# A Mamba-like block with a mixture of experts: the router's mean in halves, eight tokens normalised by ScalarE, and batch 0's LN turned by quarters

## The chip, the cores and the metric

The kernel runs on one core of a Trainium2 chip. The time is the device time of one execution in microseconds (us), the median of several runs. The engines are TensorE (PE, with its weight loads PEld), VectorE (DVE), ScalarE (ACT), GpSimd (POOL), and SyncE (SP), which issues the DMAs. Each engine runs its own instructions in their order; semaphores (`wait_ge`, `then_inc`) tie them together.

## The reference

Two batches (B = 2) of S = 2048 tokens, DM = 256, inner width DI = 512, H = 32 heads, all float32. Cut to what matters:

```python
xn   = rmsnorm(layernorm(x)) * rms_w
z, K, V = split(xn @ in_proj_W.T + in_proj_b)          # V: 512 wide, K: 512 x 2
u    = silu(causal_conv4(V) + conv_b)
coefficients = f(u @ dyn_W, seldt_W, selB, selC, beta, rg, ug)   # 11 x 32 columns per token
S_t  = rotate(S_{t-1}) + beta * (v - k . rotate(S_{t-1})) * k     # a scan over the tokens
y    = groupnorm(sum(Q * S_t)) * silu(z) + D * u
x1   = x + layernorm(layernorm(x) + y @ out_W.T)
# the experts, two of eight for each batch
x2   = layernorm(x1)
top2 = top_k(mean_over_tokens(x2) @ Wr, 2);  w = softmax(top2)
out  = x1 + layernorm(sum_e w_e * (gelu(x2 @ W1_e + b1_e) @ W2_e + b2_e))
```

## The kernel before

**Layout.** Token 16c + j of a batch lies in partition c, column j: a batch is L = 16 tiles j of 128 tokens, four of which make a quarter n (NCH = 4). V and u lie transposed in `uT`, four groups g of 128 channels; a "tile of V" is one (n, g), 512 columns, NV = 16 of them, made in the order VORD, which begins with quarters 3 and 0 of group 0, because the causal taps of quarter 0 need the last columns of quarter 3.

**Batch 0's start.** DVE makes the first statistics (`x_stats`) and in `normed_x` (L1219) centres and scales each token tile into `x_c`; PE turns it (two 128x128 transposes, L486); ACT evicts the first half of the channels (L826) and DVE the second (L1236). PE's `values` (L489) waits until all is turned. ACT's `values_and_u` (L839) evicts each tile of V twice (tap 3 of the convolution into `uT`, V itself into `vbuf`); DVE adds taps 2, 1 and 0 (`convolution`, L1263); ACT takes SiLU (`silu_u`); PE multiplies each token tile by 352 columns (`head_projections`, L528), and DVE evicts these head tiles (`head_tile`, L1313), 0 to 7 inside the convolution's loops and 8 to 15 as `tile(0)` to `tile(7)` inside `heads_half`.

**Work for batch 1 done ahead, in batch 0.** DVE takes statistics of batch 1's x (`x_ahead`), ACT the two roots (`root_ahead`), normalises the tiles (ACT's `x_ahead`), PE turns them and makes V (`values_ahead`, L502), ACT evicts (`turned_ahead` L883, `v_ahead` L890); both go to memory and come back when batch 1 starts. Where these steps stand in ACT's order is written out by hand in ACT's `heads` (L926), between the steps of the head arithmetic that DVE waits for. `fixed_steps` (L921) is softplus of a constant row; `key_bias` (L829) writes the bias of a key into its psum banks.

**Heads and scan.** DVE's `heads_half` (L1332) runs twice and hands square roots, logarithms and the like to ACT through `hd_vec` and `hd_act`. `pass_1` (L1515) goes through 16 keys backwards with 2 x 2 updates; PE makes the keys (`key`, L553) and turned tokens (`token_u`, L542). `chunk_scan` joins the 128 chunks; `turn_ends` (L592) and `turn_starts` (L614) turn its input and output on PE; `pass_2` (L1709) goes forward with the queries.

**Output and router.** `gates_and_norms` (ACT L1020, DVE L1789) gates y by quarters, adds the projection, takes the LN, adds x, and takes the next LN's statistics; ACT takes the roots (`block_root`), DVE normalises (`normed`, L1846). `mean_x2` (L703) sums x2 over the tokens on PE as a product of 1/std with x1. `router` (L720) turns x2 on PE in between; ACT evicts the turned tiles (L1065); DVE's `choose` (L1887) picks the experts and `expert_weights` (L1901) makes their softmax and copies it to all partitions (`wbc`).

**Experts.** Batch b's 64 expert units (NF; one is `up`, L746, four passes of 512 columns, with a Gelu of ACT, L1089, and `down`, L760, eight passes of 256) are spread: batch 0's run in the gaps of batch 1's attention, at places named by the constants UF = 4, UM = 7, US = 9, UH = 12 and the list UNITS; after `turn_ends` the units from UNITS[16] to 63 follow, and then the queries. Batch 1's 64 units end the kernel. SP loads the weights of two units at a time into a ring of four, in the order of the same constants. PE's order at the end of batch 1's scan:

```python
                keys(b)
                turn_ends(b)
                if b > 0:
                    experts(b - 1, UNITS[L], NF)
                    pe.wait_ge(f_used, b * NCH)
                queries(b)
```

## Time and profile before

| | us |
|---|---|
| median of 3 runs | 1499.26 (1498.65 to 1499.3) |
| the profiled execution | 1499.28 |
| its span, first to last instruction | 1497.2 |
| PE busy | 1263.3 (84%) |
| DVE busy | 1170.8 (78%) |
| ACT busy | 528.0 (35%) |
| POOL busy | 174.0 (12%) |
| mean granted TensorE clock | 0.943 of full |

Stages by the timeline: batch 0's projections and heads to about 156 us, its scan and queries to 543, its output and router to 614; batch 1's the same to 735, 1185 and 1256; batch 1's experts to 1487, and the last normalisation. A row of the timeline gives the start, the busy time of a group of like instructions, engine, line and operation, output and input, and in brackets the engine's idle time before it and what ended that. The profile ascribes a wait to the semaphore that came last.

### The profile page before, as it was taken

The page shows a single profiled execution, that of the slowest core. Times are in us where ns is not written, and L with a number is a line of the kernel's source. Part 1 is how long each engine was busy: PE and PEld are TensorE (multiplying, and loading weights), DVE is VectorE, ACT ScalarE, POOL GpSimd, SP SyncE. Part 2 cuts the span into 40 slices and gives each one's busy share as a digit, 9 for nine tenths or more (in the row PEclk, how much of TensorE's full clock was granted, in tenths as well). Part 3 has the DMA queues.
Part 4 walks back from the last instruction along what each step waited for, and adds up shares of the span by engine and source line. Part 5 has one row for each costly group of instructions (what it writes and reads, how often), then busy time and mean ns, then how long its engine had stood idle before and what let it go on. Part 6 is the DMA issues. An engine that isn't in the chain of part 4 may idle for free. (4 is left out here: it accounts for less than half of the span.)

```text
span 1497.2 us, 13142 instructions
## 1 busy us (share of the span) xinstructions
PE 1263.3 (84%) x4248; PEld 747.8 (50%) x4248; DVE 1170.8 (78%) x1906; ACT 528.0 (35%) x1196; POOL 174.0 (12%) x77
## 2 busy tenths in 40 slices
PE   5978688763898779697999899599997797999997
PEld 2454233332445446354665555465554474666664
DVE  5888999988999978859899999869999775610011
ACT  3877110100113255467432223221223554332332
POOL 0000144410222200000011111001221100000000
PEclk9998899986999999799999999799999898999999
DMA  6003111010211120700223231212111103332221
GB/s 225 1 8 140 71 57 56 28 56 0 99 57 46 40 104 22 267 21 29 71 84 99 85 99 56 84 71 98 44 55 42 56 1 121 142 129 70 85 70 70
DMA packets 54389, 110.79 MB, mean 74 GB/s; under 512 B 4785, under 2 KB 40114, under 8 KB 52274
## 3 DMA queue, kind: packets, MB, share of 16 engines
q1 hardware_dynamic: 54322, 109.97, 20.6%
q8 instruction: 34, 0.56, 0.2%
q14 instruction: 33, 0.27, 0.1%
HBM read 81.64 MB, written 28.31 MB: 73 GB/s over the span
## 5 line engine op out<-in xcount | busy, mean ns | idle before, releaser
L760 PE MATMUL ps<-kz 128*128 128x256 f32 x1024 | 245.8, 384 | 18.8 <-ACT kz L1089 14.2
L760 PEld LDWEIGHTS ps<-kz 128*128 128x128 f32 x1024 | 195.8, 192 | 103.3 <-issue 62.5
L746 PE MATMUL ps<-kz 128*128 128x512 f32 x512 | 245.6, 603 | 0.3 <-DVE small L1909 0.3
L638 PE MATMUL ps<-wshare,uT 128*128 128x512 f32 x512 | 225.8, 594 | 0.0
L1089 ACT ACTIVATE kz<-ps,small 128x512 f32<-128x512 f32 x128 | 87.3, 685 | 280.0 <-PE ps L746 279.8
L638 PEld LDWEIGHTS ps<-wshare,uT 128*128 128x128 f32 x512 | 95.4, 191 | 108.7 <-issue 108.7
L558 PE MATMUL ps<-wshare,xnT 128*128 128x512 f32 x256 | 119.9, 612 | 30.0 <-ACT ps L837 29.9
L1148 POOL TENSOR_TENSOR work<-work 128x1024 f32<-128x1024 f32 x28 | 66.9, 2391 | 620.3 <-DVE work L1610 372.5
L746 PEld LDWEIGHTS ps<-kz 128*128 128x128 f32 x512 | 99.3, 195 | 79.3 <-issue 73.1
L990 ACT ACTIVATE kz<-ps 128x128 f32<-128x128 f32 x128 | 33.7, 278 | 288.6 <-PE ps L629 288.6
L1921 DVE TENSOR_TENSOR kz<-ps,b_s 128x256 f32<-128x256 f32 x16 | 6.3, 413 | 135.9 <-PE ps L760 135.9
L1165 POOL TENSOR_TENSOR kz<-work 128x1024 f32<-128x1024 f32 x30 | 71.6, 2386 | 308.2 <-DVE work L1741 308.2
L837 ACT ACTIVATE ps<-bk_s 128x1024 f32<-128x1024 f32 x32 | 32.8, 1026 | 171.6 <-DVE wshare L1531 171.6
L629 PE MATMUL ps<-ident,kz 128*128 128x128 f32 x512 | 69.3, 294 | 26.2 <-DVE kz L1722 26.2
L629 PEld LDWEIGHTS ps<-ident,kz 128*128 128x128 f32 x512 | 67.8, 208 | 42.3 <-DVE kz L1722 29.9
L558 PEld LDWEIGHTS ps<-wshare,xnT 128*128 128x128 f32 x256 | 47.3, 194 | 82.5 <-issue 47.6
L538 PE MATMUL ps<-wshare,uT 128*128 128x352 f32 x256 | 79.4, 473 | 2.9 <-ACT uT L855 2.9
L1706 DVE TENSOR_TENSOR work<-ps,coef 128x1024 f32<-128x1024 f32 x60 | 70.5, 1216 | 1.4 <-PE ps L638 1.4
L538 PEld LDWEIGHTS ps<-wshare,uT 128*128 128x128 f32 x256 | 50.1, 196 | 32.0 <-ACT uT L855 3.5
L674 PE MATMUL ps<-xnT,wz_s 128*128 128x512 f32 x128 | 61.5, 628 | 5.3 <-ACT work L1018 5.3
L550 PE MATMUL ps<-ident,uT 128*128 128x128 f32 x256 | 40.5, 283 | 30.1 <-DVE wshare L1718 16.3
L569 PE MATMUL ps<-work,nident 128*128 128x512 f32 x112 | 54.5, 631 | 10.7 <-DVE work L1627 10.7
(292 smaller groups left out, 2037.4 us busy)
## 6 DMA issues: line engine op xcount, KB each, us to landing
kz<-in_w SPq DMA_DIRECT2D x128, 256.0 KB, 2.9
kap_d<-kz SPq DMA_DIRECT2D x26, 512.0 KB, 2.7
kz<-kap_d SPq DMA_DIRECT2D x26, 512.0 KB, 3.3
kz<-in_x SPq DMA_DIRECT2D x3, 2048.0 KB, 8.0
v_d<-kz SPq DMA_DIRECT2D x4, 1024.0 KB, 4.4
wshare<-in_wq SPq DMA_DIRECT2D x2, 2048.0 KB, 7.6
coef<-in_x SPq DMA_DIRECT2D x2, 2048.0 KB, 7.9
work<-v_d SPq DMA_DIRECT2D x3, 1024.0 KB, 7.0
```

The lines of the kernel that those rows point to most:

```text
L538: t = mm(ps[:, sm_bank(b, j), 0:NSM * H], uT3[:, k, j * P:(j + 1) * P], wsm_s[:, k, :], start=(k == 0), stop=(k == KI - 1))
L558: t = mm(ps[:, k_bank(b, i) + c, :], xnT[:, k, j * P:(j + 1) * P], wk_s[:, k, c, :], start=False, stop=(k == KM - 1), skip_group_check=True)
L569: t = mm(ps[:, 4 + 2 * a + c, :], ident[:] if i == 0 else nident[:], X[:, a, c], start=(i == 0), stop=True, skip_group_check=True)
L629: t = mm(ps[:, 6 + j % 2, g * P:(g + 1) * P], qb(j)[:, i, g * P:(g + 1) * P], ident[:], start=(i == 0), stop=(i == 1))
L638: t = mm(ps[:, 2 * (j % 2) + c, :], uT3[:, k, j * P:(j + 1) * P], wq_s[:, k, c, :], start=(k == 0), stop=(k == KI - 1))
L674: t = mm(ps[:, i % 4, :], wz_s[:, k, g * P:(g + 1) * P], xnT[:, k, n * 512:(n + 1) * 512], start=(k == 0), stop=(k == KM - 1))
L746: t = mm(ps[:, 4 + i % 2, :], w1_r[r][:, k, (f % 2) * P:(f % 2 + 1) * P], x2T[:, k, n * 512:(n + 1) * 512], start=(k == 0), stop=(k == KM ...
L760: t = mm(ps[:, 6 + q // 2, (q % 2) * DM:(q % 2 + 1) * DM], hbuf(i)[:, q * P:(q + 1) * P], w2_r[r][:, f % 2, :], start=(f == 0 and q % 2 == ...
L1089: af(hbuf(i), ps[:, 4 + i % 2, :], ACT.Gelu, bias=b1_s[:, f // FT, f % FT:f % FT + 1]).then_inc(h_done, 1)
L1148: nc.gpsimd.tensor_tensor(PSt[:, :, 2], PSt[:, :, 2], Z, ALU.add).then_inc(sum_ready, 1)
L1165: nc.gpsimd.tensor_tensor(qb(j), w[0], w[1], ALU.add).then_inc(turned_ready, 1)
L1706: t = tt(w, q, wide(cf[:, H_ + i:H_ + i + 3:2, j]), MUL)
```

## The change

It has these parts, all of order and placement; what is computed is the same.

- Batch 0's x is centred in the order of quarters 3, 0, 1, 2 and turned by half-quarters (four transposes into one psum bank); ACT evicts all eight of them, DVE none. V's first two products start after quarters 3 and 0, then come the other turns. V's weights have a semaphore of their own.
- ACT: `fixed_steps` and `key_bias(b, 0)` come after `silu_u(2)`, no longer before `root_ahead(1)`.
- Heads: DVE's `tile(0)`, `tile(1)` stand ahead of the wait for rope, `tile(6)`, `tile(7)` ahead of L1400; ACT's steps for batch 1 are placed anew (`x_ahead(5, 12)`, `turned_ahead(0, 6)` in the first half, `turned_ahead(6, 8)`, `v_ahead(2, 6)` and `v_ahead(6, 10)` in the second). In batch 1 the Gelu of unit 7 comes before the squares.
- Batch 1's start: tap 3 of quarter 0 is ACT's, made at the end of batch 0's norms; `expert_weights` stands inside DVE's first taps instead of after them.
- Units 9 to 11 come after the first key and the first turned tokens. UNITS[16] is 57, not 54: units 54 to 56 move from behind `turn_ends` into the last step of the keys, and unit 57 between the two turned ends.
- Output and router: x1's statistics of tokens tiles 0 to 7 get a root of their own, ACT normalises these eight (x2a_ready) and DVE the other eight; the mean's products run in bank 3 in three groups (0, 8, 12), ahead of the wait for o_used.

The diff, cut to its core:

```diff
...
-UNITS = [15] + [15 + 12 * i // 5 for i in range(L - 1)] + [54]
+UNITS = [15] + [15 + 12 * i // 5 for i in range(L - 1)] + [57]
...
+        XORD = (3, 0, 1, 2)
...
+            def turned_x(first, last):
+                for t in range(first, last):
+                    n, k = XORD[t // 2], t % 2
+                    pe.wait_ge(xc_ready, 4 * (t // 2) + 4)
+                    if t >= 4:
+                        pe.wait_ge(xt_done, t - 3)
+                    for q in range(4):
+                        r = tr(ps[:, 4 + t % 4, q * P:(q + 1) * P], x_c[:, 4 * n + q, k * P:(k + 1) * P], ident[:])
+                    r.then_inc(xt_ready, 1)
+
+            def values():
+                turned_x(0, 4)
+                pe.wait_ge(wv_loaded, 16)
+                for i in range(NV):
                     n, g = VORD[i]
+                    if i == 2:
+                        turned_x(4, 8)
+                    pe.wait_ge(xt_done, (2, 4)[i] if i < 2 else 4 if i < 8 else 8)
...
                 for o in range(2):
+                    if b > 0 and o:
+                        experts(b - 1, UNITS[L], UNITS[L] + 1)
                     pe.wait_ge(end_ready, b * 2 + o + 1)
...
             def mean_x2(b):
+                pe.wait_ge(sz_ready, b * NV + NV)
+                for j in range(L):
+                    if j in (0, 8, 12):
+                        pe.wait_ge(ln_ready, b * 3 + 1 + (0, 8, 12).index(j))
+                    mm(ps[0:1, 3, 0:DM], rs2[:, j:j + 1], x1_tok[:, j], start=(j == 0), stop=(j == L - 1))
                 pe.wait_ge(o_used, b * L + L)
-                for j in range(L):
-                    if j % 12 == 0:
-                        pe.wait_ge(ln_ready, b * 2 + 1 + j // 12)
-                    mm(ps[0:1, 4, 0:DM], rs2[:, j:j + 1], x1_tok[:, j], start=(j == 0), stop=(j == L - 1))
...
                     clean_banks(b)
-                    experts(b - 1, UM, UH)
+                    experts(b - 1, UM, US)
                     pe.wait_ge(xnp_loaded, 16)
                 key(b, 0)
                 token_u(b, 0, L - 1)
+                if b > 0:
+                    experts(b - 1, US, UH)
...
                 if b > 0:
-                    experts(b - 1, UNITS[L], NF)
+                    experts(b - 1, UNITS[L] + 1, NF)
                     pe.wait_ge(f_used, b * NCH)
...
                 for i in range(NV):
                     value(i)
+                    if i == 1:
+                        turned_x(4, 8)
                     if i == 11:
                         silu_u(0)
-                if b == 0:
-                    act.wait_ge(consts_loaded, 16 * 7)
-                    fixed_steps()
-                key_bias(b, 0)
                 root_ahead(1)
                 silu_u(1)
                 root_ahead(2)
                 silu_u(2)
+                act.wait_ge(consts_loaded, 16 * 7)
+                fixed_steps()
+                key_bias(b, 0)
                 silu_u(3)
...
                         x_ahead(0, 5)
                     elif b == 0:
-                        turned_ahead()
+                        turned_ahead(6, 8)
                         v_ahead(0, 2)
+                    elif h == 1:
+                        experts(b - 1, UM, UM + 1)
...
                     if b > 0 and h == 1:
                         key_bias(b, 0)
-                        experts(b - 1, UM, US)
+                        experts(b - 1, UM + 1, US)
                     elif b == 0 and h == 0:
-                        x_ahead(5, 9)
+                        x_ahead(5, 12)
                     elif b == 0:
-                        v_ahead(2, 4)
+                        v_ahead(2, 6)
...
-                    if b == 0 and h == 0:
-                        x_ahead(9, 12)
-                    elif b == 0:
-                        v_ahead(4, 6)
...
                         x_ahead(12, L)
+                        turned_ahead(0, 6)
                     else:
-                        v_ahead(6, 9)
+                        v_ahead(6, 10)
...
+                def x2_normed(first, last):
+                    act.wait_ge(ln_ready, b * 3 + 1)
+                    for j in range(first, last):
+                        af(r_tok[:, j], x1_tok[:, j], ACT.Identity, scale=rs2[:, j:j + 1], bias=nb[:, j:j + 1]
+                           ).then_inc(x2a_ready, 1)
...
                 normed(3)
-                block_root(6, slice(12, L))
+                x2_normed(0, 3)
+                block_root(7, slice(12, L))
+                x2_normed(3, 8)
+                if b + 1 < B:
+                    act.wait_ge(y2_ready, b * NV + NV)
+                    taps(b + 1, 0)
...
-                for j in range(L + 2):
-                    if j < L:
+                for n in XORD:
+                    for j in range(4 * n, 4 * n + 4):
                         tsc(x_c[:, j, :], x_in[:, j, :], mv[:, j, 0:1], t2[:, j:j + 1], SUB, MUL).then_inc(xc_ready, 1)
-                    if j >= 2:
-                        dve.wait_ge(xt_ready, b * L + j - 1)
-                        tsc(xnT[:, 1, (j - 2) * P:(j - 1) * P], ps[:, 6 + j % 2, 0:P],
-                            col[:, C_RMS + 1:C_RMS + 2], None, MUL).then_inc(xt_copied, 1)
...
-                    for k in (2, 1, 0):
+                    for k in (2, 1, 0) if b == 0 else ():
...
+                        if n == 0 and k == 2:
+                            expert_weights(b - 1)
...
                 tile(5)
+                tile(6)
+                tile(7)
                 dve.wait_ge(hd_act, a0 + 7)
...
-                summed(1)
+                part_moments(4, summed(1), slice(0, 8))
                 scaled(3, 2)
+                part_scale(4, slice(0, 8)).then_inc(ln_ready, 1)
...
```

## Rows read from the trace of the kernel before

**Rows 1.** The page: busy time, share of the span and instructions of each engine.

```profile
PE 1263.3 (84%) x4248; PEld 747.8 (50%) x4248; DVE 1170.8 (78%) x1906; ACT 528.0 (35%) x1196; POOL 174.0 (12%) x77
```

**Rows 2.** Waits of VectorE: line, releaser, us in total, times, longest.

```profile
DVE kz L1921 <- PE ps L760: 135.9, 4, 41.0
```

**Rows 3.** Timeline of batch 0's start: centring, turning, V.

```profile
14.46 1.06 DVE L1233 TENSOR_SCALAR uT<-uT,small 128x256 f32<-128x256 f32 x3
...
15.02 9.61 PE L486 MATMUL ps<-ident,uT 128*128 128x128 f32 x32 [15.02 <-DVE uT L1233]
...
25.16 6.40 PE L498 MATMUL ps<-xnT,wshare 128*128 128x512 f32 x10 [0.54 <-ACT xnT L826]
...
28.95 0.78 ACT L845 ACTIVATE uT<-ps,small,col 128x512 f32<-128x512 f32 x1 [3.92 <-PE ps L498]
...
48.99 5.74 PE L498 MATMUL ps<-xnT,wshare 128*128 128x512 f32 x13
```

**Rows 4.** Timeline of batch 0's first steps on ACT and DVE after V.

```profile
57.60 0.27 ACT L922 ACTIVATE small<-dtc_s 128x32 f32<-128x32 f32 x1
...
61.98 1.28 ACT L874 ACT_TABLE_LOAD   x1
...
63.68 0.25 DVE L1252 RECIPROCAL pre<-small 128x16 f32<-128x16 f32 x1 [4.47 <-ACT small L874]
...
82.11 2.62 ACT L855 ACTIVATE uT<-uT 128x512 f32<-128x512 f32 x4 [7.85 <-DVE uT L1182]
```

**Rows 5.** Timeline of batch 0's heads.

```profile
110.29 3.68 PE L510 MATMUL ps<-ident,kz 128*128 128x128 f32 x16 [7.58 <-DVE coef L1317]
...
119.53 4.33 ACT L887 ACTIVATE kz<-ps,col 128x512 f32<-128x512 f32 x7
...
129.27 0.43 DVE L1370 TENSOR_TENSOR work<-work 128x256 f32<-128x256 f32 x1 [3.67 <-ACT work L946]
...
137.31 1.75 DVE L1400 RECIPROCAL work<-work 128x256 f32<-128x256 f32 x1 [1.81 <-ACT work L963]
```

**Rows 6.** Timeline of batch 0's router and batch 1's start.

```profile
601.36 9.24 PE L708 MATMUL ps<-coef,small 128*1 128x256 f32 x32 [5.90 <-DVE small L1182]
...
605.90 4.18 PEld L708 LDWEIGHTS ps<-coef,small 128*1 128x1 f32 x20 [0.20 <-issue]
...
606.28 3.96 DVE L1848 TENSOR_SCALAR kz<-coef,small 128x256 f32<-128x256 f32 x12
...
618.51 0.33 SPq L368 DMA_DIRECT2D b_s<-in_b  x1
...
618.60 2.21 ACT L900 ACTIVATE uT<-work,col 128x512 f32<-128x512 f32 x3
...
627.36 0.16 DVE L1909 COPY small<-ps 128x2 f32<-128x2 f32 x1 [0.74 <-PE ps L734]
...
649.68 0.53 DVE L1317 TENSOR_TENSOR coef<-ps,bsm_s 128x352 f32<-128x352 f32 x1 [14.09 <-PE ps L538]
```

**Rows 7.** Timeline of the second key of batch 1.

```profile
740.46 3.60 PE L558 MATMUL ps<-wshare,xnT 128*128 128x512 f32 x8
...
744.16 1.23 DVE L1529 TENSOR_TENSOR wshare<-ps,coef 128x1024 f32<-128x1024 f32 x1 [4.73 <-PE ps L558]
```

**Rows 8.** Timeline from the last key of batch 1 to its queries.

```profile
952.90 2.79 PE L610 MATMUL ps<-ident,work 128*128 128x128 f32 x12 [12.13 <-DVE work L1653]
...
959.88 2.79 PE L610 MATMUL ps<-ident,work 128*128 128x128 f32 x12 [4.19 <-ACT work L983]
...
966.77 1.88 PE L746 MATMUL ps<-kz 128*128 128x512 f32 x4
...
970.22 1.88 PE L746 MATMUL ps<-kz 128*128 128x512 f32 x4
...
1001.52 0.69 DVE L1718 TENSOR_TENSOR work<-ps,coef 128x512 f32<-128x512 f32 x1 [6.23 <-PE ps L550]
...
1009.26 1.23 DVE L1726 COPY work<-ps 128x1024 f32<-128x1024 f32 x1 [7.05 <-PE ps L618]
```

More of the change, by code:

```diff
@@ L823, in normed_x, with turned_x @@
                 root(b, 2, t1, t0, eps6)
[L824 to L827 removed]
+                turned_x(0, 4)
+            def turned_x(first, last):
+                for t in range(first, last):
+                    n, k = XORD[t // 2], t % 2
+                    act.wait_ge(xt_ready, t + 1)
+                    af(xnT[:, k, n * 512:(n + 1) * 512], ps[:, 4 + t % 4, :], ACT.Copy,
+                       scale=col[:, C_RMS + k:C_RMS + k + 1]).then_inc(xt_done, 1)
             def key_bias(b, i):
@@ L881, in x_ahead, with turned_ahead @@
                     af(x_p[:, j], x_p[:, j], ACT.Identity, scale=t2[:, j:j + 1], bias=t0[:, j:j + 1]).then_inc(xnp_ready, 1)
-            def turned_ahead():
-                for i in range(2 * NCH):
+            def turned_ahead(first, last):
+                for i in range(first, last):
                     n, k = i // 2, i % 2
@@ L1289, in convolution @@
                     x_ahead(0)
-                else:
-                    expert_weights(b - 1)
-                for n in range(1, NCH):
+                for n in range(1 if b == 0 else 0, NCH):
                     if b == 0:
```

114 lines of the change are left out of this document (49 added, 65 removed).

## The prediction

> **What bounds the kernel now.** I read the waits of VectorE first, then walked the timeline at each wait that an edit touches. VectorE (DVE) is busy for 78% of the span, TensorE (PE) for 84%, and neither is the bound throughout [rows 1]. From the start to the end of batch 1's attention the work hangs on DVE's order, and after it 64 expert units of batch 1 run at PE's pace (DVE waits 135.9 us for them [rows 2]). So a microsecond that DVE is spared before about 1250 us is worth one if no other engine is late in its place; the last stretch is unchanged and only starts earlier. DVE's waits ahead of it, and what each edit moves, are the timeline rows of the stages [rows 3 to 8]. The profiled execution took 1499.28 us, its span 1497.2, so 2.1 lie outside; the median is 1499.26, so the sum made on the span holds for the median.
>
> **A. Batch 0's start.** Today the centring of a token tile alternates on DVE with a copy of the turned half, so 16 tiles are turned from 15.0 to 24.6 us, and V's products begin at 25.16 and end at 54.7 [rows 3]. After the change DVE only centres: three in a row took 1.06 us, some 0.33 each, so quarter 3 is ready at 15.8 and quarter 0 at 17.2. PE turns four half-quarters: 16 turns took 3.68 us in the later stage [rows 5], so 3.9 us with latency, to 19.8. ScalarE (ACT) evicts each in about 0.65 (seven took 4.33 [rows 5]) behind it. V's first two tiles then take 3.4 us plus a cold start, the other 16 turns 3.7, the 14 remaining tiles 1.72 each (four passes, 0.43 apart; thirteen end to end took 5.74 [rows 3]): 19.9 + 3.4 + 1.2 + 3.7 + 24.1 = 52.3, against 54.7. Gain 2.4 us on PE and about as much on DVE, whose convolution follows V tile by tile. The cold start: ACT takes V's first tile 3.79 us after its products begin [rows 3], twice the later pace: the row of 1.2 GHz against that of 2.4, and it costs V about 1.7 us. I take 1.2 of it, with 0 and 1.7 as ends.
>
> The Trainium skill (TensorE: Matmul & The Clock Gate, Part 1: The HAM clock gate) says that the array's slow clock is the default and that activity releases it. By it the unbroken turns would have released it before V starts, and A would be worth 1.2 us more; in today's trace the turns are as many but spaced by DVE, and V began slow.
>
> Next, ACT makes fixed_steps and key_bias before the root that DVE needs: from 57.60 to 61.98, 4.38 us, and DVE waits 4.47 [rows 4]. Moved behind silu_u(2), they fall into ACT's 7.85 us of idle time ahead of silu_u(3) [rows 4]; with one more load of Silu's table (1.28) they take 5.7, so they stay hidden. If the cover were gone, silu_u(3) would be late by what overhangs, and PE wants its output only some 4 us later. Late next: ACT, which ends the four tiles of V that silu_u(0) held up at 55.3 (57.6 today, 2.3 less), then table 1.28 and root 0.31; DVE's reciprocal at 57.3 instead of 63.7. **A = 6.4 us** (ends 4 and 7.7), the 2.4 included.
>
> **B. Batch 0's heads.** tile(6) and tile(7) stand ahead of L1400. Their psum tiles are ready by then, and sm_done's 16th count releases PE's turns for batch 1 seven microseconds sooner than 110.29 [rows 5]. ACT then evicts six of the eight ahead of the second half's first steps, instead of seven in a run from 119.53 that holds up the squares: DVE waits 3.67 for them [rows 5]. Only two evictions and two V tiles stay there, ending near 122, and DVE comes at 125.6: all 3.67 go. The V evictions taken from between Ln and Sqrt let Sqrt's table load run under DVE: of the 1.81 us at L1400 [rows 5] 0.7 to 1.5 go, since V's tiles 2 and 3 may come slowly after PE's pause. In the first half nothing is won: the same 12 x_ahead calls and table loads stand on ACT, and tiles 6 and 7 fill a 0.7 us wait that comes back at Ln. Moving tiles 0 and 1 ahead of the rope wait fills one wait, but the next, on ACT's Ln, ends the same. **B = 4.8** (3 and 5.2).
>
> **C. Router and batch 1's start.** The mean's 32 passes ran from 601.36 to 610.6: the last 20 took 4.2, 0.21 each, the 12 before them some 0.4 each [rows 6]. That, with DVE's 14 of 16 normed tiles (12 took 3.96 us, 0.33 each [rows 6]), sets the router. Now 16 passes run in o's wake, 8 after ln_ready 2, 8 after ln_ready 3. DVE gets a further set of moments and scale (about 1.2 us) and loses 8 tiles (2.6), so ends 1.4 earlier; the last 8 passes begin at about 607.2 and end at 608.9, or 610.6 if the clock has fallen in the pauses. I take 0.6 us for each batch (ends -0.5 and 1.7).
>
> Then the large wait: DVE stands 14.09 us until head tile 0 [rows 6]. PE does four expert units first, and these wait for wbc, copied at 627.36 [rows 6], and for ACT. Now tap 3 of quarter 0 is ACT's (four calls, 2.9 us: three of L900 take 2.21 [rows 6]) and expert_weights stands behind the first taps, so wbc comes when PE's turns and the Exp are done. ACT's eight tiles at 0.51 and four taps end at 612.3, its evictions at 618.3, wbc at 618.9. ACT's taps(1) end at 621.2, but it then waits for the experts' biases: issued at 618.51 [rows 6], 3 to 5 us to land. The two Gelus end near 627.5 where they ended at 634.7; all that follows on ACT and PE keeps its lengths, so head tile 0 comes 7.0 us sooner, and 7 us of the wait remain. That wait also covers DVE's own 2.6 us saving in the convolution, which is worth nothing. ACT's new work is hidden until about 612; uncovered it would cost up to 7 us. **C = 7.0** (3 and 8.6), with batch 0's 0.6 in it.
>
> **D. Start of batch 1's scan.** The key comes ahead of units 9 to 11. DVE waits 4.73 us for the second key, whose products ran from 740.46 [rows 7]. PE reaches it sooner, but it needs key_bias(1), and that needs DVE's first rotation, done near 737.7: key 1 can end near 742.5. Unit 7's Gelu fits ACT's idle time before the squares. **D = 1.4** (0 and 2.9).
>
> **E. Units moved ahead of the queries.** A unit is 3.45 us (L746 to L746 [rows 8]). PE is idle for 12.13 us before the first ends are turned and 4.19 before the second [rows 8]: three units (10.3) and one (3.4) fit. Six instead of ten stay behind, so PE reaches the queries 13.8 us sooner, at 987.5. Today DVE is through with its scan at 995.3 (1001.52 less 6.23), waits 6.23 for the tokens and 7.05 for the start states [rows 8]. After: query 0 ends at 994, turn_starts follows scan_done (994.4, some 0.9 before output_bias is through), DVE goes on at 996.0 instead of 1009.26, and query 1 is due about when DVE wants it. SP's queue: the loads of pairs 27 to 31 now stand ahead of wq's, the last waits for unit 55, near 951, and wq is due at 987. **E = 13.4** (10 and 13.8).
>
> **F. Batch 1's router.** Only the 0.6 of C; idx, the weight and bias loads and the first Gelu follow it. **F = 0.6.**
>
> Sum: 6.4 + 4.8 + 7.0 + 1.4 + 13.4 + 0.6 = 33.6; 1497.2 - 33.6 + 2.1 = 1465.7 us. With all low ends 19.5 (1479.8), with all high ends 39.9 (1459.4).
>
> **Rivals.** (1) The boundary turns into ACT's: eight more normed tiles and four taps stand ahead of the evictions of the turned tokens, which today begin just after the mean, near 611. If they begin 3 us later than I have it, or the biases and weights land late, C falls to 3 and F to 0: 33.6 - 4.0 - 0.6 = 29.0, and 1497.2 - 29.0 + 2.1 = 1470.3. For it: ACT has 7 us more there. Against it: today ACT has nothing to do between its last root and the first eviction, nor between the last tap and the first unit, which begins with wbc. Chance 0.2. (2) The end units don't come free, E = 0: unit 56's Gelu stands in ACT's order ahead of the copies of mt; if it comes late, the whole chunk scan does. Then 1479.1. Against: PE was idle for the whole gap [rows 8], and ACT, which waits there for the same ends, too. Chance 0.05. (3) Clock, the rule named in A: A with V at full clock, both routers at 1.7: 33.6 + 1.2 + 2.2 = 37.0, 1462.3. Chance 0.15. (4) Slower: SP's queue. The five new pair loads block it until PE has done unit 55. If PE stood on a weight of those units, wq's load would come late, and with it the queries. E turns into a loss only if wq lands after 1001, and the kernel is slower only if that is 20 us later still, at 1021, which is wq issued near 1013 instead of 952.8: 1502 and more. Against: PE takes 6.9 us for a pair, and nowhere in today's list of its waits does it stand for a weight load. Chance 0.02.
>
> **How the numbers follow.** The forecast has 0.58, its own range 1461 to 1470. The range that should hold 8 in 10 reaches to rival 3's 1462 with its bounds and past rival 1: 1459 to 1475. Less than 0.2% (3 us) can hardly be told from no change in a measurement of this kernel; nothing but parts lost nearly whole would leave that: 0.01. Slower 0.02, faster 0.97.
>
> **What would show it.** A: first V product near 20, L1252 near 57. B: no wait at the second L1370. C: wbc near 619, wait at head tile 0 down to 7 us. D: L1529's wait near 3.3. E: no idle gap between unit 53 and the first turned ends, L1726 within 2 us of scan_done. The last stretch still at 3.45 per unit. Wrong if the biases land late, if ACT's order at the boundary binds, or if PE's clock falls in the new pauses.

## The result and the profile after

The changed kernel took 1458.72 us (median of 4: 1454.36, 1457.01, 1460.44, 1461.17) against 1499.28 for the four runs of the kernel before beside it: 40.5 us less, ratio 0.9728 with a 95% interval of 0.9714 to 0.9742. A second set of five runs, beside the kernel before on another occasion, gave 1459.11 and 0.9725 (0.9712 to 0.9738). I had forecast 1465.7 with a range of 1459 to 1475: the direction was right, and the kernel came out 7 us faster than the forecast and 0.3 us below the range.

The profiled execution took 1460.44 us. Its page, busy time of each engine and the granted TensorE clock in 40 slices of 36.5 us:

```profile
span 1458.7 us, 13147 instructions
PE 1254.9 (86%) x4248; PEld 741.9 (51%) x4248; DVE 1160.4 (80%) x1886; ACT 538.2 (37%) x1211; POOL 174.0 (12%) x77
PEclk9998999976999989999999999999998899999999
```

VectorE lost 10.4 us of work and PE 8.4 of busy time [rows 1 has the page of before]; neither is where the 38.5 us of span went. The last stretch is unchanged, as foreseen: DVE waits 135.9 us for the units, to the digit the row of before [rows 2].

```profile
DVE kz L1944 <- PE ps L769: 135.9, 4, 41.0
```

So everything is gained ahead of batch 1's experts. I took the start time of the same DVE instruction in both traces, stage by stage; how much sooner each stands says what each step brought (line numbers are those of the changed kernel, up to some 30 higher than before; the differences are of unrounded times; in brackets what I had foreseen):

| mark on DVE | before | after | sooner | step |
|---|---|---|---|---|
| reciprocal of batch 1's early LN (L1276) | 63.68 | 53.72 | 9.97 | A: 6.4 foreseen |
| second head step (L1392) | 129.27 | 115.15 | 14.1 | B: 4.8 foreseen, 4.2 here, 3.0 to 3.4 at the next steps |
| group norm of batch 0 | 544.31 | 534.41 | 9.90 | 3.0 lost, not foreseen |
| router of batch 0 (L1914) | 610.67 | 599.56 | 11.12 | C's router: 1.2 (0.6) |
| head tile 0 of batch 1 (L1339) | 649.68 | 628.06 | 21.63 | C in all: 11.7 (7.0) |
| second key of batch 1 (L1551) | 744.16 | 720.99 | 23.18 | D: 1.5 (1.4) |
| start states copied (pass_2) | 1009.26 | 971.88 | 37.38 | E: 13.0 (13.4), after 1.2 at the turned ends |
| router of batch 1 (L1914) | 1252.69 | 1214.04 | 38.65 | F: 1.7 (0.6), after 0.5 lost ahead of it at batch 1's group norm |

The timeline of the changed kernel's start, PE and ACT (start, duration, engine, line, operation, count, and idle time before it with what ended it), beside [rows 3]:

```profile
16.02 3.65 PE L487 MATMUL ps<-ident,uT 128*128 128x128 f32 x16 [16.02 <-DVE uT L1261]
19.46 3.75 PE L501 MATMUL ps<-xnT,wshare 128*128 128x512 f32 x8
21.53 0.78 ACT L860 ACTIVATE uT<-ps,small,col 128x512 f32<-128x512 f32 x1 [1.14 <-PE ps L501]
23.05 1.91 PE L487 MATMUL ps<-ident,uT 128*128 128x128 f32 x16
24.79 24.20 PE L501 MATMUL ps<-xnT,wshare 128*128 128x512 f32 x56
```

The second sixteen turns took 1.91 us, half of what the first sixteen took and half of the 3.7 that I had priced. V starts at 19.46 (19.9 foreseen) and ends at 49.0, not 52.3. The boundary between the batches, beside [rows 6]:

```profile
607.15 0.38 PE L743 MATMUL ps<-small,onerow 1*128 1x2 f32 x2 [0.78 <-DVE small L1929]
607.63 0.16 DVE L1932 COPY small<-ps 128x2 f32<-128x2 f32 x1 [0.54 <-PE ps L743]
607.85 3.70 PE L755 MATMUL ps<-kz 128*128 128x512 f32 x8 [0.32 <-DVE small L1932]
611.28 0.72 ACT L1113 ACTIVATE kz<-kz,small 128x512 f32<-128x512 f32 x1 [1.60 <-DMA b_s<-in_b]
623.56 1.99 PE L769 MATMUL ps<-kz 128*128 128x256 f32 x8 [0.87 <-ACT kz L1117]
628.06 0.53 DVE L1339 TENSOR_TENSOR coef<-ps,bsm_s 128x352 f32<-128x352 f32 x1 [6.89 <-PE ps L541]
```

The weights (wbc, L1932) come 19.7 us sooner than at 627.36, and PE has waited only 0.78 us for them where it had stood still for 9.19. The wait at head tile 0 is 6.89 us. What I had not priced is in the third line: the first two up projections took 3.70 us, where the same eight passes before had taken 6.42:

```profile
626.67 0.58 PE L734 MATMUL ps<-small,onerow 1*128 1x2 f32 x2 [9.19 <-DVE small L1906]
627.58 6.42 PE L746 MATMUL ps<-kz 128*128 128x512 f32 x8 [0.32 <-DVE small L1909]
643.70 3.48 PE L760 MATMUL ps<-kz 128*128 128x256 f32 x8 [2.81 <-ACT kz L1089]
```

Both surpluses are the same instructions in less time, by a factor of 1.9 and 1.7, and TensorE's two clock levels stand in the ratio of two. That was the theory to be tested: **the terms that I mis-sized are those in which the new order has PE busy just before a stage, so that the stage starts at 2.4 GHz instead of 1.2.** It held for A's turns, in part for the router, and not for C. The rival: the surplus is other engines' earlier work and transfers, and the clock is a bystander.

### The profile page after: what moved, and what is told of

Its sections match the earlier page's. It is cut to its first block and busy times, and to the rows that moved or that the text cites. A ratio compares the mean times of both kernels' runs of the same rounds, so it can differ in the third digit from the quotient of the medians.

```text
span 1458.7 us, 13147 instructions
## 1 busy us (share of the span) xinstructions
PE 1254.9 (86%) x4248; PEld 741.9 (51%) x4248; DVE 1160.4 (80%) x1886; ACT 538.2 (37%) x1211; POOL 174.0 (12%) x77
## 5 line engine op out<-in xcount | busy, mean ns | idle before, releaser
L1005 ACT ACTIVATE kz<-ps 128x128 f32<-128x128 f32 x128 | 33.6, 277 | 290.5 <-PE ps L634 290.5
L1944 DVE TENSOR_TENSOR kz<-ps,b_s 128x256 f32<-128x256 f32 x16 | 6.3, 414 | 135.9 <-PE ps L769 135.9
L541 PE MATMUL ps<-wshare,uT 128*128 128x352 f32 x256 | 76.3, 459 | 1.7 <-DVE coef L1339 1.7
```

The lines of the kernel that those rows point to most:

```text
L541: t = mm(ps[:, sm_bank(b, j), 0:NSM * H], uT3[:, k, j * P:(j + 1) * P], wsm_s[:, k, :], start=(k == 0), stop=(k == KI - 1))
```

## The experiments

Each was timed five times (e12 twelve times) beside the kernel before, whose medians were 1500.71, 1500.2 and 1500.6 in the three sets. A loss against the changed kernel is the difference of the two ratios times 1500, with 0.9726 for the changed kernel; it is uncertain by some 3 us. Each kernel has one profile, and a profile is of one run: those of e2, e3 and e7 are of their fastest run. Idle products are matrix products that write to a free psum bank and that nobody reads.

**e1: the kernel before, PE kept busy in the 9.2 us ahead of the weights.** This adds work whose results nobody uses, and leaves all other work where it was.

```diff
                 turn_x2(b, 4, 8 if b == B - 1 else L)
+                if b < B - 1:
+                    pe.wait_ge(x2t_done, b * L + L)
+                    fill(5, 3)                      # 5 idle products of 256 columns, bank 3
+                    pe.wait_ge(conv_done, (b + 1) * NV + 2)
+                    fill(5, 3)
+                    pe.wait_ge(conv_done, (b + 1) * NV + 3)
+                    fill(5, 3)
                 pe.wait_ge(wrow_ready, b + 1)
```

> The kernel before, with three groups of five idle products of 256 columns on TensorE (each as long as a warm 0.43 us; nobody reads them) laid into its 9.2 us of waiting for the router's weights, so that it is busy when the first expert units of batch 0 come. Theory (the boundary's surplus over my C is TensorE's clock): the granted clock of 627 to 634 us, 0.57 before, comes near 1, the first two up projections take 3.7 us instead of 6.42, ScalarE's wait for them shrinks alike, head tile 0 of batch 1 and the end come 2.7 us sooner: 1496.6. If the products themselves run slow they end up to 3 us late, and the kernel loses that instead. Rival (the surplus is ScalarE's and the transfers' earlier work): the same time as before, 1499.3.

Measured: 1495.19 us, ratio 0.9964 (0.9951 to 0.9978): 5.4 us faster (3.3 to 7.4), from work that computes nothing. Busy time by stretch of the kernel before and then of e1 (the columns: PE, PEld, DVE, ACT, POOL busy us, PEclk, DMA share, GB/s):

```profile
618.00:627.00 9.00, 0.33 (x2) 0.33 (x2) 8.27 (x16) 2.81 (x5) 0.00 (x0) 0.58 0.86 270
627.00:634.00 7.00, 6.68 (x11) 3.02 (x11) 6.60 (x11) 2.69 (x3) 0.00 (x0) 0.57 0.90 377
```

```profile
618.00:627.00 9.00, 7.08 (x31) 5.44 (x30) 8.11 (x17) 2.40 (x4) 0.00 (x0) 1.00 0.86 285
627.00:634.00 7.00, 7.00 (x23) 4.03 (x22) 7.00 (x12) 5.97 (x9) 0.00 (x0) 1.00 0.80 338
```

The granted clock of 627 to 634 us goes from 0.57 to 1.00, and e1's chain reads:

```profile
626.54 3.70 PE L757 MATMUL ps<-kz 128*128 128x512 f32 x8 [0.32 <-DVE small L1920]
639.95 1.99 PE L771 MATMUL ps<-kz 128*128 128x256 f32 x8 [2.82 <-ACT kz L1100]
644.45 0.53 DVE L1328 TENSOR_TENSOR coef<-ps,bsm_s 128x352 f32<-128x352 f32 x1 [9.88 <-PE ps L538]
```

Head tile 0 stands 5.24 us sooner than at 649.68: 2.7 from the two ups, 1.5 from the third unit's down projection (1.99 for 3.48 after the same idle 2.8 us), 0.2 from the small product that carries the weights, warm too (0.38 for 0.58); 0.8 stood already at the router, ahead of the idle products. The 1.5 can't be put down to the idle products. In the profile of e12, a kernel with this boundary as before and nothing laid into it, the same rows are:

```profile
627.45 5.09 PE L746 MATMUL ps<-kz 128*128 128x512 f32 x8 [0.32 <-DVE small L1906]
642.24 2.00 PE L760 MATMUL ps<-kz 128*128 128x256 f32 x8 [2.82 <-ACT kz L1086]
```

The down projection was fast there too, and the ups took 5.09. So in place the filling is worth 1.6 to 2.9 us, the ups and the small product, and the 2.7 that I had priced lies in between. Why the gain of the medians lies above it stays open. The Trainium skill (TensorE: Matmul & The Clock Gate, Loop structure matters more than you think) sets dense PE work against a long wait for a DMA ahead of every matmul, after which the array runs at its slow clock; in the kernel before the wait is for DVE, 9.19 us, and the granted clock behind it was 0.57, which agrees.

**e2 and e3: idle products in the changed kernel.** e2 has 28 turns of the identity ahead of batch 0's first turn, e3 four products of 256 columns in each pause of the mean and four ahead of the last turned y tile.

```diff
             def values():
+                for i in range(28):
+                    tr(ps[:, i % 4, 0:P], ident[:], ident[:])
                 turned_x(0, 4)
```

```diff
                     if j in (8, 12):
+                        fill(4, 0)
...
                 gate_tile(b, 2)
+                fill(4, 3)
                 turn_y(b, L - 1)
```

> The changed kernel, with 28 idle turns of the identity on TensorE ahead of batch 0's first turn, from the landing of the identity at about 10 us to about 15. Theory: the first 16 turns then take 1.9 us, as the second 16 do, instead of 3.65, and V starts up to 1.7 us sooner than 19.46; ScalarE's evictions of 0.69 us each, 0.86 apart today, take part of it back. DVE's wait ends sooner by that, and the end comes 0.5 to 1.7 us sooner: 1457. Rival (the slow turns are VectorE's pace in centring): no change, 1458.7.

> The changed kernel, with four idle products of 256 columns in each of the two pauses of the mean over tokens (both batches) and four in the pause ahead of the last turned y tile of each batch. Theory: the pause of 2.98 us is where TensorE's clock fell in the changed kernel and not in the one before; filled, the last turned y takes 2.05 us instead of 3.78 and the gates behind it 3.60 instead of 4.76, batch 0's group norm comes 3 us sooner, and the third part of the mean takes 1.9 us instead of 3.24 in either batch: together 3 to 6 us sooner, 1453 to 1456. Rival (the later group norm is ScalarE's or VectorE's work): within 1 us of 1458.7, or slower by what the idle products overhang.

Measured: e2 1460.85, ratio 0.9732 (0.9713 to 0.9752); e3 1459.48, ratio 0.9724 (0.971 to 0.9739): no difference from the changed kernel in either. Yet each did in place what was expected of it. e2's start:

```profile
9.52 4.60 PE L492 MATMUL ps<-ident 128*128 128x128 f32 x28 [9.52 <-DMA col<-in_cols]
16.10 1.09 PE L487 MATMUL ps<-ident,uT 128*128 128x128 f32 x8 [1.98 <-DVE uT L1263]
18.32 3.60 PE L503 MATMUL ps<-xnT,wshare 128*128 128x512 f32 x8
```

Eight turns took 1.09 us, 0.14 each instead of 0.23, V began 1.1 us sooner, and DVE's first step of the convolution 1.3 (23.34 for 24.64). The 28 idle turns themselves wait for nothing but the first: the first twelve stand 0.21 us apart and the last fifteen 0.11, so it is PE's own earlier work that halves them, and not DVE's pace. In e3's profile both later parts of batch 0's mean took 1.89 us (3.24 for the last one in the changed kernel), and the last turned y 2.05. But e2's profile, with no idle product there, shows the last turned y at 2.05 as well, so e3 can't claim that. Both profiles are of the fastest run (1452.38 for e2, whose median is 1460.85, and 1454.47 for e3), so they don't say what the middle run did. The gains in place are real in these profiles; in the medians they can't be told from the spread between executions, to which e9 turns.

**e4: the end units undone (E).**

```diff
-UNITS = ... + [57]
+UNITS = ... + [54]
                 for o in range(2):
-                    if b > 0 and o:
-                        experts(b - 1, UNITS[L], UNITS[L] + 1)
...
-                    experts(b - 1, UNITS[L] + 1, NF)
+                    experts(b - 1, UNITS[L], NF)
```

> The changed kernel with ten units instead of six behind the turned ends, as before (54 in the table, no unit between the two ends). My prediction's E: 13.4 us (10 to 13.8) come back, 1472. Rival (the units don't come free): under 5 us, below 1464.

Measured: 1472.04, ratio 0.9811 (0.9798 to 0.9824): 12.7 us lost. PE's rows of the changed kernel and then of e4 around the turned ends:

```profile
926.02 1.89 PE L769 MATMUL ps<-kz 128*128 128x256 f32 x8
929.70 1.50 PE L615 MATMUL ps<-ident,work 128*128 128x128 f32 x12 [1.79 <-DVE work L1675]
...
936.69 1.61 PE L615 MATMUL ps<-ident,work 128*128 128x128 f32 x12 [2.04 <-ACT work L998]
```

```profile
937.17 2.79 PE L613 MATMUL ps<-ident,work 128*128 128x128 f32 x12 [4.19 <-ACT work L996]
986.70 1.22 DVE L1746 COPY work<-ps 128x1024 f32<-128x1024 f32 x1 [7.05 <-PE ps L621]
```

E is what I said, four units moved into idle time: the start states come 14.8 us later without it. 1.7 of that stand already at the chunk scan, 0.5 from earlier stages and 1.2 from its second twelve turns, which took 2.79 us instead of 1.61. That 1.2 is the clock that the units keep up, and not their place.

**e5: batch 0's turns undone (the larger part of A).** XORD, `turned_x`, the four evictions by ACT and their semaphores go back to the loop of before.

```diff
-                for n in XORD:
-                    for j in range(4 * n, 4 * n + 4):
-                        tsc(x_c[:, j, :], ...).then_inc(xc_ready, 1)
+                for j in range(L + 2):
+                    if j < L:
+                        tsc(x_c[:, j, :], ...).then_inc(xc_ready, 1)
+                    if j >= 2:
+                        dve.wait_ge(xt_ready, b * L + j - 1)
+                        tsc(xnT[:, 1, ...], ps[:, 6 + j % 2, 0:P], ...).then_inc(xt_copied, 1)
```

> The changed kernel with batch 0's normalisation turned token tile by token tile again, half of it evicted by VectorE, as before; all else changed. My prediction's price for this part of A: V ends 2.4 us later, 1461.1. Theory (the part that I mis-sized, since V's first products ran warm and the second 16 turns took 1.91 us instead of the 3.7 priced): 5 to 6 us later, as V's end (54.7 against 48.8 us), 1464.3. Rival (V's earlier end is lost again behind other waits of batch 0): under 1 us, below 1459.7.

Measured: 1468.29, ratio 0.9778 (0.9762 to 0.9795): 7.8 us lost, 2.4 foreseen in the sum and 5 to 6 by the theory. The mark on DVE is 6.3 us later from 36 us on, and 6.3 to 6.6 to the last norms at 1230. PE then turns in one spaced run and V starts slow, as before [rows 3]:

```profile
15.38 9.61 PE L487 MATMUL ps<-ident,uT 128*128 128x128 f32 x32 [15.38 <-DVE uT L1253]
29.32 0.78 ACT L854 ACTIVATE uT<-ps,small,col 128x512 f32<-128x512 f32 x1 [3.92 <-PE ps L499]
```

**e6: the taps and the weights' place undone (C without the router).**

```diff
-                if b + 1 < B:
-                    act.wait_ge(y2_ready, b * NV + NV)
-                    taps(b + 1, 0)
...
+                    if b > 0:
+                        t = mark(tsc(acc(0, g), vbuf[g][:, 3:7, :], ...))
...
-                        if n == 0 and k == 2:
-                            expert_weights(b - 1)
```

> The changed kernel with batch 1's first quarter convolved by VectorE alone again and the experts' weights computed behind all of it, as before; the mean in its new order stays. My prediction's price (C without the router): 6.4 us, 1465.1. Theory: TensorE then waits some 9 us for the weights again, its granted clock falls and the first two up projections take 6.42 us instead of 3.70: 10 to 11 us, 1469.5. Rival (the surplus came from the mean's new order): under 5 us, below 1463.7.

Measured: 1467.29, ratio 0.9773 (0.9757 to 0.9788): 7.0 us lost, close to the 6.4 of my sum and not the 10 to 11 of the theory. Its rows:

```profile
616.10 0.16 DVE L1931 COPY small<-ps 128x2 f32<-128x2 f32 x1 [0.74 <-PE ps L743]
616.32 5.70 PE L755 MATMUL ps<-kz 128*128 128x512 f32 x8 [0.32 <-DVE small L1931]
631.73 1.99 PE L769 MATMUL ps<-kz 128*128 128x256 f32 x8 [2.82 <-ACT kz L1114]
636.22 0.53 DVE L1338 TENSOR_TENSOR coef<-ps,bsm_s 128x352 f32<-128x352 f32 x1 [11.89 <-PE ps L541]
```

The slow ups are back (5.70), as the theory has it, but they aren't worth what I thought. From the copy of the weights to head tile 0 it is 22.3 us in the kernel before, 20.1 in e6, 20.4 in the changed kernel and 18.1 in e1. The changed kernel has warm ups and gains nothing by them: they end at 611.5, and the Gelu behind them waits for the experts' biases, which landed at 611.28, 3.65 us after the weights. In e1 the biases are long there and the warmth counts. So the theory fell for C. Its surplus of 4.7 us (11.7 less 7.0) is 1.4 us of weights sooner than I had them, and 3.3 between weights and head tile, where I had 23.8 us (642.7 less 618.9). Of the 3.3, some 1.7 lie ahead of the end of the first two Gelus, 6.9 us behind the weights where I had 8.6: I had left the issue of the biases at 618.51, and it moved with the router to 607.31. The other 1.5 is the third unit's down projection, at the fast clock in the changed kernel, in e6 and, with the old boundary, in e12.

**e7: the router's order undone.**

```diff
-                pe.wait_ge(sz_ready, b * NV + NV)
+                pe.wait_ge(o_used, b * L + L)
                 for j in range(L):
-                    if j in (0, 8, 12):
-                        pe.wait_ge(ln_ready, b * 3 + 1 + (0, 8, 12).index(j))
+                    if j % 12 == 0:
+                        pe.wait_ge(ln_ready, b * 2 + 1 + j // 12)
...
-                x2_normed(0, 3)
-                block_root(7, slice(12, L))
-                x2_normed(3, 8)
+                block_root(6, slice(12, L))
```

> The changed kernel with the mean over tokens in its old order (twelve tiles, then four, behind the output's evictions) and all 16 tiles normalised by VectorE, in both batches; ScalarE's taps stay. My prediction's price: 0.6 us for each batch, 1459.9. Theory (the surplus of the router lies in the mean's passes at the slow clock, 0.4 us each): 1.2 us in batch 0 and 2.0 to 2.7 in batch 1, 1462.4. Rival (ScalarE's eight tiles delay its evictions): 0 or a gain, 1458.7 or less.

Measured: 1463.33, ratio 0.9761 (0.9748 to 0.9775): 5.2 us lost, where the sum had 1.2 and the theory 3.7. From DVE's last mark ahead of the changed order to the router it is 0.5 us in batch 0 and 2.6 in batch 1, 3.1 together (against e9's profile 1.8 and 2.6). DVE's own work there is 1.8 us shorter in either batch, where I had 1.4; what differs is its wait for PE at the router, 0.42 us in e7 and 1.76 in the changed kernel in batch 0, 1.15 and 0.40 in batch 1. Of batch 1, e7's mean and then the changed kernel's:

```profile
1203.53 9.95 PE L712 MATMUL ps<-coef,small 128*1 128x256 f32 x32 [5.88 <-DVE small L1195]
```

```profile
1207.24 3.27 PE L713 MATMUL ps<-coef,small 128*1 128x256 f32 x8 [2.99 <-DVE small L1210]
1212.07 1.89 PE L713 MATMUL ps<-coef,small 128*1 128x256 f32 x8 [1.56 <-DVE small L1210]
```

In the old order all 32 passes follow a pause of 5.88 us, and the granted clock was 0.57 from 1202 to 1210. In the new one the first sixteen run warm behind the output products (3.61 us from 1200.64), eight behind a pause at 0.41 us each, and the last eight warm. So the clock is worth 0.75 us of the 2.6 here. In batch 0 of the first profile it was the last eight that ran slow (3.24 us, at 596.23), which took back 1.3 of the 1.8 that DVE had saved.

**e8 and e12: batch 0's heads (B), undone in the changed kernel and done alone in the kernel before.** The edit moves `tile(6)` and `tile(7)`, the rope wait, and the places of `x_ahead`, `turned_ahead` and `v_ahead`, back or forth:

```diff
-                        turned_ahead(6, 8)
+                        turned_ahead()
                         v_ahead(0, 2)
...
                         x_ahead(12, L)
-                        turned_ahead(0, 6)
...
-                tile(6)
-                tile(7)
```

> The changed kernel with batch 0's heads in their old order (all eight turned tiles in one run in the second half, tiles 6 and 7 behind the first half's last steps). My prediction's B: 4.8 us, 1463.5. By the traces' stage marks 3.0 to 4.1, 1462.3. Rival (the order is hidden): under 1 us.

> The kernel before with only the new order of batch 0's heads. Prediction's B: 4.8 us, 1495.4 against 1500.2. The stage marks with this part undone in the changed kernel: 3.7 us at the end of the heads, 1496.5; the times there: 7.6 us, 1492.6. If the parts don't add up because of TensorE's clock, this one gives 3 to 4 here where it gave 7.6 there.

Measured: e8 1466.69, ratio 0.9779 (0.9765 to 0.9793): 7.9 us lost; e12 1496.46, ratio 0.9976 (0.9965 to 0.9986): 3.6 us won. In place both are near each other: at L1418, inside the second half, e8 is 3.74 us later and e12 3.0 sooner, at L1424 4.1 and 3.4. What e8 loses beyond that comes later, at places that the edit doesn't touch: 1.6 more at 823 us, 1.1 at 940, 1.9 near the end. But that is against the first profile of the changed kernel. Against its second one (e9, below) e8 is 4.9 us later at 200 us and still 5.3 at 1140: the loss at 823 and 940 stands in the unedited kernel as well, and only what comes behind 1150 us, 4.4 us, is left. e12 in turn loses 3 us at batch 0's group norm and wins 2.8 at the boundary, both where PE ran at the other clock than in the kernel before.

**e10: the fixed steps undone (the rest of A).**

```diff
+                act.wait_ge(consts_loaded, 16 * 7)
+                fixed_steps()
+                key_bias(b, 0)
                 root_ahead(1)
                 silu_u(1)
                 root_ahead(2)
                 silu_u(2)
-                act.wait_ge(consts_loaded, 16 * 7)
-                fixed_steps()
-                key_bias(b, 0)
```

> The changed kernel with the fixed steps and the first key bias ahead of the root that VectorE needs, as before. Prediction and theory agree on the direct loss: 4.4 us on ScalarE less 0.3 of slack, 4.1 at the next reciprocal, 1462.8. Rival (undone parts also move TensorE's clock further on, since four undone parts cost 26.7 us together where my sum has 15.0): 6 us and more, 1465.

Measured: 1462.95, ratio 0.9758 (0.9736 to 0.978): 4.8 us lost, 4.60 at the next reciprocal. This part of A stands as foreseen.

**e9: the changed kernel again, unedited.**

> The changed kernel once more, unedited, for a second profile of it. Its runs so far lie 6.8 us apart (1454.4 to 1461.2). Theory: the same instructions run at another of TensorE's two clocks from one execution to the next; then the stage marks of the two profiles stand apart only where a stretch has another granted clock, in steps of 1 to 3 us, and a run's time follows its mean clock: near 1454 at 0.960, near 1461 at 0.955. Rival (the memory or the other engines): marks apart where a transfer or an activation ends the wait, at an equal clock.

Measured: 1459.11 (1458.07 to 1459.89). Its profile differs from the first one although no instruction does. The end of batch 0's second pass in the first profile and then in this one:

```profile
525.84 3.78 PE L634 MATMUL ps<-ident,kz 128*128 128x128 f32 x16 [2.98 <-DVE kz L1744]
529.42 4.76 PE L679 MATMUL ps<-xnT,wz_s 128*128 128x512 f32 x8
532.14 0.29 DVE L1784 TENSOR_REDUCE small<-small 128x8 f32<-128x128 f32 x1 [6.36 <-ACT ps L1010]
```

```profile
524.60 2.05 PE L634 MATMUL ps<-ident,kz 128*128 128x128 f32 x16 [2.98 <-DVE kz L1744]
526.48 3.60 PE L679 MATMUL ps<-xnT,wz_s 128*128 128x512 f32 x8
529.17 0.29 DVE L1784 TENSOR_REDUCE small<-small 128x8 f32<-128x128 f32 x1 [4.63 <-ACT ps L1010]
```

The same sixteen turns, after the same 2.98 us of idle time, ran at the slow clock once and at the fast clock once; the granted clock of the stretch around the gates behind them was 0.64 and 1.00. It goes the other way at 814, again first profile, then this one:

```profile
816.38 1.97 PE L769 MATMUL ps<-kz 128*128 128x256 f32 x8 [2.97 <-ACT kz L1101]
```

```profile
814.53 3.75 PE L769 MATMUL ps<-kz 128*128 128x256 f32 x8 [2.96 <-ACT kz L1101]
823.43 1.23 DVE L1551 TENSOR_TENSOR wshare<-ps,coef 128x1024 f32<-128x1024 f32 x1 [1.57 <-PE ps L561]
```

Here this profile gives back 1.6 us, and DVE's wait of 1.57 is new. From 534 to 940 us the marks go from 4.1 sooner to 0.9 later. Between the executions of one kernel the time goes roughly with the mean clock, e3's for one: 1454.47 and 1455.7 us at 0.962, 1459.48 at 0.958, 1460.38 at 0.957, 1460.65 at 0.956. It is no strict rule: I had expected some 1461 at 0.955, and e9's five runs, all at 0.955, took 1458.07 to 1459.89, less than the first set's 1461.17 at 0.957. And V began cold in this profile:

```profile
19.37 4.82 PE L501 MATMUL ps<-xnT,wshare 128*128 128x512 f32 x8
```

That is 1.07 us more than the 3.75 of the first profile, and DVE's convolution starts 1.0 later. The clock at 525 us is also the 3.0 us that the comparison of before and after shows as lost at the end of batch 0's second pass, since before's profile had the fast clock there. The rival, transfers or activations, has no row at the two marks shown: each waits for PE, directly or through ACT, and only PE's durations differ.

**e11: every pause filled that I knew of.** e2's and e3's idle products, but five (batch 0) or eight (batch 1) instead of four before the last turned y, and five between the first up and down projections.

```diff
                 gate_tile(b, 2)
+                fill(8 if b else 5, 3)
                 turn_y(b, L - 1)
...
                     up(i)
+                    if i == 1:
+                        fill(5, 6)
```

> The changed kernel with idle products in every pause of TensorE that a wait of VectorE or ScalarE hangs on and that I know of: 28 turns ahead of batch 0's start, four products of 256 columns in each pause of either mean, five and eight ahead of the last turned y, five between the first up and down projections of either batch. Theory: 1.3 at the start, up to 3 at each end of the second pass, 1.3 to 1.5 in each mean, 1.5 at the third unit: all runs at the fast end of the changed kernel's, 1451 to 1454. Rival (what clock the shorter pauses leave is decided elsewhere): 1457 to 1460, as the kernel with half of these products, 1459.5.

Measured: 1457.25 (1454.58 to 1458.85), ratio 0.9713 (0.9698 to 0.9728). That is 2 us under the changed kernel, with intervals that overlap: the rival's 1457 to 1460, and not the 1451 to 1454 of the theory. Its profile is 5.9 us ahead of the first one at 534 us, and 0.9 ahead at 940: its granted clock from 780 to 820 us was 0.91 where the first profile has 1.00 and e9's, with nothing laid anywhere, 0.92. Filling some of the pauses did not remove the slow stretches elsewhere.

## Why the prediction was off, step by step

| part | foreseen | at the marks | whole kernel |
|---|---|---|---|
| A, turns | 2.4 | 6.3 (e5) | 7.8 |
| A, fixed steps | 4.0 | 4.6 (e10) | 4.8 |
| B | 4.8 | 3.7 (e8), 3.9 (e12) | 7.9 undone, 3.6 alone |
| C, taps and weights | 6.4 | 8.2 (e6) | 7.0 |
| router, both batches | 1.2 | 3.1 (e7) | 5.2 |
| D | 1.4 | 1.5 | not tried |
| E | 13.4 | 13.1 (e4) | 12.7 |
| sum | 33.6 | 40.5 | 40.5 measured |

The marks are differences of single profiles, good to one or two us: against e9's profile A's turns are 5.4, the router 4.4 and B 4.9. That their sum meets the measured 40.5 to the digit is luck.

- **Bound and stages**: right. The last stretch is unchanged, and what was won ahead of it arrived: 38.65 us at batch 1's router, 38.5 at the end of the span.
- **A**: the mechanism was right and two terms were mis-sized. I priced the turns with 3.68 us for sixteen, a row of [rows 5], for turns that would run in the midst of V's products: 1.91 us measured. The granted clock of the stretch that row comes from was 0.62, as this line of the kernel before shows (columns as above), and the sum had not used it:

```profile
110.00:124.00 14.00, 7.33 (x33) 6.96 (x34) 13.24 (x44) 11.25 (x15) 0.00 (x0) 0.62 0.00 0
```

 And I took 1.2 us of cold start for V, where in this profile the turns just ahead had warmed it: 3.75 us for its first two tiles. Of the 3.3 us by which V ends sooner than foreseen, the turns are 1.9, the cold start 1.0 and V's earlier start 0.4; e5's V ends another 0.6 later than the kernel before's (55.3 for 54.7), which makes the 3.9 between 2.4 and 6.3. The sentence on the Trainium skill in A (TensorE: Matmul & The Clock Gate, Part 1) had V starting at the fast clock; the first profile agrees, while in e3's the same eight passes took 4.42 and in e9's, the same kernel, 4.82. So my 1.2 was wrong for one execution of this kernel and nearly right for another; the price of the turns was wrong in both (1.91). One caution: the profile's granted clock can't confirm the cold start. It reads 1.00 for the kernel before while V's first products stand 0.86 us apart, because its record has no entry before 28.9 us (19.8 in the changed kernel):

```profile
25.00:28.00 3.00, 2.84 (x4) 1.31 (x5) 0.47 (x8) 0.03 (x1) 0.00 (x0) 1.00 0.00 0
```

 That it is the clock is read from the factor of two on the same passes, and from e2.
- **B**: 1.1 us too high by the first profile. DVE's wait of 3.67 at that step is gone, but a new one of 1.03 came at L1418, where there had been none and I had named none, and the one at L1424 for the square root is still 1.45 of 1.81 [rows 5], where I had 0.7 to 1.5 of it go:

```profile
122.07 0.42 DVE L1418 TENSOR_TENSOR work<-work,coef 128x256 f32<-128x256 f32 x1 [1.03 <-ACT work L975]
123.94 1.75 DVE L1424 RECIPROCAL work<-work 128x256 f32<-128x256 f32 x1 [1.45 <-ACT work L977]
```

- **C**: the wait of 6.89 at head tile 0 equals the 7 foreseen only by an error of mine. Of the 11.7 us, 7.2 are less waiting and 4.5 are DVE's own earlier arrival; the latter I had counted as worth nothing, and it would have lengthened the wait had the units come when I said. The surplus is in the weights (1.4 us) and behind them (3.3): the biases, whose issue I had left at its old time, came sooner, and the third unit ran at the fast clock. The warm ups gave nothing, since the biases' landing, which I had named, still ended the wait. Against the part undone (e6) the surplus is 1.8.
- **Router and F**: the term was mis-sized. I gave 0.6 us to each batch, between -0.5 with the last passes slow and 1.7 with them fast, and had DVE's part 1.4 shorter. Measured against the order undone it is 0.5 and 2.6, in before against after, counted from the group norm, 1.2 and 1.7: DVE's part is 1.8 shorter, and in batch 1 the last eight passes ran at the fast clock (1.89 us), so that it counted; in batch 0 of the first profile they did not (3.24). This is rival 3, the clock, which I gave 0.15. It had 3.4 for the two routers, near the 3.1 measured; its 1462.3 was nearer than my forecast and still not far enough, because it too kept the second turns at 3.7 us.
- **D, E**: right to 0.4 us. SP's queue (rival 4) and the units' price (rival 2) left no trace; nor did rival 1: ACT's evictions at the boundary began at 600.63, a microsecond after the first turn, and not later than I had them.
- **The range**: its low end had all the high ends of the terms in it, 39.9 us. It did not allow for the clock of later stages, which moved the marks of two executions of one kernel against each other by 5 us between 534 and 940 us. In view of the nine executions of the changed kernel (1454.4 to 1461.2), 0.3 us below the range means nothing; the 7 us against the forecast do. By part they are A's turns (+3.9), the router (+1.9), C (+1.8) and the fixed steps (+0.6), less 1.1 for B and 0.2 for D and E, 6.9 in all.

The step of the prediction that failed is, first of all, A's sum for the end of V, which had sixteen turns at 3.7 us between V's products, from a row at the slow clock: they took 1.91, and V ended at 49.0 and not 52.3. After it come the 0.6 for each router and C's units and biases, which I let come too late. The first is shown by the rows and by e5; for the router and C the rows name the cause, and no run isolates it.

What stays open: what decides the clock after a pause of just under 3 us. The rows show it both ways at equal pauses, and no edit here settled it. Nor is it shown why undoing B costs 7.9 us where B alone brings 3.6, a difference of 4.3 that is uncertain by 3; I have one profile of e8. And of e1's 5.4 us only 1.6 to 2.9 are accounted for.

## What to carry to other kernels

Before you price a PE step that is moved, read the granted clock of the stretch from which its row comes, and ask what PE does just before the step's new place: my largest error, A's turns, was a row of the slow clock used for a place that was warm, a factor of two. An edit that puts dense PE work ahead of a latency chain can be worth more than its instructions, but only where nothing else, such as a DMA, ends the wait next: C's warm ups gave nothing. A tool for it is cheap: idle products in one pause (e1) show what its clock costs. And before you read a difference of a few us from two profiles, take a second profile of the same kernel (e9): it moved the marks by up to 5 us.

## What the runs showed of the hardware that I had not expected

- An unedited kernel ran the same instructions after the same idle time (2.98 and 2.98 us; 2.97 and 2.96 us) at either clock level in different executions: 3.78 or 2.05 us for sixteen turns, 1.97 or 3.75 for eight products of 256 columns. Each of the two moved DVE's marks, by 3.0 and 1.6 us. The nine runs of this kernel lie 6.8 us apart, 0.5%; that such changes make up all of this spread is likely and not shown.
- Work that computes nothing made the kernel before faster by 5.4 us, 3.3 to 7.4 (e1); spread over many pauses of the changed kernel it won 2, within the uncertainty (e11).
- PE's own earlier work sets the pace of its turns: with nothing to wait for, the first twelve idle turns of e2 stand 0.21 us apart and the last fifteen 0.11.

Six parts undone one at a time cost 45.4 us in all, against the 40.5 of the whole change. The sum is uncertain by some 10 us, since each loss is taken from the same two measurements of the changed kernel, so it doesn't show that the parts fail to add up.
